# Top two of the gate with copy and guard on VectorE, and the output products of one layer in one slot

## Reference

```python
x = x + 0.5 * ffn(layernorm(x))      # first layer ("b" in the kernel)
x = x + attn(layernorm(x))           # attention
x = x + 0.5 * ffn(layernorm(x))      # second layer ("a" in the kernel)
```

```python
logits = normalize(h) @ normalize(sim) - sigmoid(gates)
gated = relu(logits)                         # experts with a positive logit are active
fallback = the 2 largest logits, where no expert is active
rw = softmax(where(active or fallback, gated, -inf))
q, k, v = (sum_e rw[e] * (h @ proj[e]) for each of the three)      # 64 wide
att = softmax(causal(q @ k.T / 8)) @ v
out = sum_e (att * rw[e]) @ o_proj[e]
```

## Time and profile before

| | |
|---|---|
| time, median of 3 runs | 4582.05 us (4581.81 to 4588.16) |
| profiled execution | 4587.97 us, its span on the core 4586.2 us |
| mean granted TensorE clock | 0.929 of full speed |
| TensorE busy (matmul) | 3939.6 us, 86% |
| VectorE busy | 4033.8 us, 88% |
| ScalarE busy | 3579.0 us, 78% |
| GpSimd busy | 3676.2 us, 80% |

### The profile page before, as it was taken

One profiled execution on the slowest core, in us unless ns is written; L12 is line 12 of the kernel. 1 busy time (PEld: TensorE's weight loads), 2 busy tenths in 40 slices (PEclk: granted clock), 3 DMA queues, 4 the chain that ended last, 5 costly groups with the idle time before them and its releaser, 6 DMA issues.

```text
span 4586.2 us, 93566 instructions
## 1 busy us (share of the span) xinstructions
PE 3939.6 (86%) x29004; PEld 3205.8 (70%) x29004; DVE 4033.8 (88%) x14021; ACT 3579.0 (78%) x9797; POOL 3676.2 (80%) x4414
## 2 busy tenths in 40 slices
PE   6678888898998899888898989888988988987777
PEld 5556777776777777777677777777777777765666
DVE  2389999989999998999999999999989899999992
ACT  2378878888887888888788878878888887877772
POOL 1567988888898888888888888988988898876650
PEclk8778999999999999999999999999999999989888
DMA  3111211112121111111112112111211111110011
GB/s 104 36 35 35 57 50 50 57 50 55 48 57 48 51 56 51 54 51 52 53 50 57 50 51 55 50 55 49 56 49 52 55 52 53 50 41 27 27 31 51
DMA packets 243941, 230.47 MB, mean 50 GB/s; under 512 B 27123, under 2 KB 176628, under 8 KB 243316
## 3 DMA queue, kind: packets, MB, share of 16 engines
q1 hardware_dynamic: 243444, 224.49, 17.5%
HBM read 214.98 MB, written 9.44 MB: 49 GB/s over the span
## 4 chain that ended last, share of the span: by engine, by line
POOL 50%; PE 20%; DVE 14%; issue 9%; ACT 6%; DMA 1%; SPq 0%; POOLq 0%; ACTq 0%; DVEq 0%
POOL HS L406 15%; POOL HL L1073 6%; POOL HL L1076 6%; POOL S L1075 6%; PE pQ L658 6%; POOL RB L419 5%; DVE M L990 4%; DVE HL L992 3%; PE pFa L602 3%; PE pST L642 2%; PE pFa L606 2%; PE pFb L626 1%; PE pO L699 1%; ACT HL L878 1%; PE pFa L544 1%
## 5 line engine op out<-in xcount | busy, mean ns | idle before, releaser
L658 PE MATMUL pQ<-wf_sb,HS 128*128 128x192 f32 x8192 | 1526.3, 343 | 196.6 <-POOL HS L406 172.4
L658 PEld LDWEIGHTS pQ<-wf_sb,HS 128*128 128x128 f32 x8192 | 1418.4, 201 | 250.2 <-POOL HS L406 151.0
L890 ACT ACTIVATE S<-S,M 128x512 f32<-128x512 f32 x1024 | 800.8, 782 | 2.9
L897 ACT ACTIVATE S<-S,lift 128x512 f32<-128x512 f32 x1024 | 787.7, 769 | 1.7 <-POOL lift L1064 1.7
L876 ACT COPY S<-pST 128x256 f32<-128x256 f32 x768 | 308.8, 402 | 456.7 <-issue 421.5
L406 POOL TENSOR_TENSOR HS<-hT_b,RB 128x1024 f32<-128x1024 f32 x240 | 575.7, 2399 | 5.0 <-PE pQ L658 3.3
L406 POOL TENSOR_TENSOR HS<-hT_a,RB 128x1024 f32<-128x1024 f32 x244 | 577.0, 2365 | 0.0
L885 ACT COPY PTs<-pST 128x512 f32<-128x512 f32 x1024 | 529.2, 615 | 4.1 <-PE pST L677 3.6
L1073 POOL TENSOR_TENSOR HL<-S,HL 128x512 f32<-128x512 f32 x384 | 491.2, 1279 | 45.6 <-ACT HL L878 45.5
L677 PE MATMUL pST<-ident,S 128*128 128x128 f32 x4096 | 508.6, 279 | 17.2 <-ACT S L873 12.4
L1075 POOL TENSOR_TENSOR S<-HL 128x512 f32<-128x512 f32 x384 | 493.1, 1284 | 30.1
(11 more groups left out here) (257 smaller groups left out, 8956.0 us busy)
## 6 DMA issues: line engine op xcount, KB each, us to landing
RB<-rows_b SPq DMA_DIRECT2D x384, 256.0 KB, 3.4
RB<-rows_a SPq DMA_DIRECT2D x384, 256.0 KB, 3.3
x_b<-in_x SPq DMA_DIRECT2D x64, 128.0 KB, 3.1
out_y<-y SPq DMA_DIRECT2D x64, 128.0 KB, 1.7
wf_sb<-in_wf SPq DMA_DIRECT2D x4, 768.0 KB, 7.0
rows_b<-rwT SPq DMA_DIRECT2D x64, 8.0 KB, 1.3
wof_sb<-in_wof SPq DMA_DIRECT2D x1, 1024.0 KB, 7.2
rows_a<-rwT SPq DMA_DIRECT2D x64, 8.0 KB, 1.4
```

What stands on the lines that cost most here:

```text
L658: mm = nc.tensor.matmul(pQ[:, 0:QKV], HS[:, k % 2, e, i, :], wf_sb[:, i, at:at + QKV], start=k + e + i == 0, stop=(k, e, i) == (3, 3, 1))
L890: nc.scalar.activation(S[:, r, :], S[:, r, :], ACT.Prelu, bias=M8[:, r, TH:TH + 1], scale=-1.0, alpha=1.0 / STEEP).then_inc(s_cut, 1)
L897: nc.scalar.activation(S[:, r, :], S[:, r, :], ACT.Exp, bias=lift[:, r:r + 1], scale=-STEEP).then_inc(s_gap, 1)
```

## The change

Pair is no longer a step of its own, and repl no longer has a slot of its own: VectorE does, in the slot of top, MAX8, the copy of the two largest (as a reduction over one element each), the guard nv (a negated maximum of the largest logit and a zero that stands in the widened buffer v8), and MATCH_REPLACE8. It waits for its own MAX8 before the copy, and for the copy before the replacement. GpSimd's gate makes one result less (four semaphore counts instead of five). For job a, TensorE issues all eight output products in slot 7; those of job b stay as they are.

```diff
@@ AT: the entries "pair" and "repl" go, for job a and for job b
-                self.v8 = sb(f"v8_{n}", P, 8)
+                self.v8 = sb(f"v8_{n}", P, 16)
...
-            if at := mine("pair"):
-                t, c = at
-                wait(eng, q["top"], t + 1)
-                ns.tensor_copy(J.mr8[:, 0:2], J.v8[:, 0:2]).then_inc(q["pair"], 1)
             if at := mine("gate"):
...
                 ns.tensor_scalar(J.pos[:], J.L[:], 0.0, None, ALU.is_gt).then_inc(g, 1)
-                ns.tensor_scalar(J.nv[:], J.v8[:, 0:1], 0.0, -1.0, ALU.max, ALU.mult).then_inc(g, 1)
-                wait(eng, g, 5 * t + 4)
+                wait(eng, g, 4 * t + 3)
...
@@ TensorE
-                if at := tile(J, "y", w, j, 1):
-                    t, c = at
-                    if isinstance(t, int) and (J.n, t) == ("b", 0):
+                if at := tile(J, "y", w, j, 1 if J.n == "b" else 0):
+                    t, c = at
+                    if J.n == "b" and t == 0:
                         pe.wait_ge(s_half, 1)
-                    wait(pe, q["read"], fill(J.n, w, j + 1))
-                    pe.wait_ge(s_mix, earlier(w, j + 1, MIXES.values()))
+                    of = j + 1 if J.n == "b" else j
+                    wait(pe, q["read"], fill(J.n, w, of))
+                    pe.wait_ge(s_mix, earlier(w, of, MIXES.values()))
                     for k in range(4):
                         nc.tensor.matmul(F[:, 0:D], RB2[:, k, :], wof_sb[:, k, :], start=k == 0, stop=False)
...
@@ VectorE, start
+                nc.vector.memset(jobs[n].v8[:], 0.0)
@@ VectorE, top
-                    nc.vector.max(J.v8[:], J.L[:]).then_inc(q["top"], 1)
-                if at := tile(J, "repl", w, j):
-                    t, c = at
-                    wait(dve, q["pair"], t + 1)
+                    nc.vector.max(J.v8[:, 0:8], J.L[:]).then_inc(q["top"], 1)
+                    dve.wait_ge(q["top"], t + 1)
+                    nc.vector.tensor_reduce(J.mr8[:, 0:2], J.v8[:, 0:2].unsqueeze(2), mybir.AxisListType.X, ALU.max
+                                            ).then_inc(q["pair"], 1)
+                    nc.vector.tensor_reduce(J.nv[:], J.v8[:, 0:16:8], mybir.AxisListType.X, ALU.max, negate=True
+                                            ).then_inc(q["guard"], 1)
+                    dve.wait_ge(q["pair"], t + 1)
                     nc.vector.match_replace(J.R[:], J.mr8[:], J.L[:], -BIG).then_inc(q["repl"], 1)
```

More of the change, by code:

```diff
@@ L62 @@
         "ctx_rec": 69, "ctx_norm": 71, "ctxT": 72, "x": 74, "x_sq": 76, "x_rstd": 77, "h": 78,
-        "hT": 79, "h_rinv": 79, "lg": 81, "shift": 82, "top": 83, "pair": 84, "repl": 85, "gate": 87,
+        "hT": 79, "h_rinv": 79, "lg": 81, "shift": 82, "top": 83, "gate": 87,
         "gate_exp": 88, "gate_em": 89, "gate_sum": 90, "rw": 91, "rwT": 92, "rw_st": 93, "hs": 96, "qkv": 104,
@@ L69 @@
         "x_ld": -51, "x_sum": -48, "x_sq": -46, "x_rstd": -45, "h": -44, "hT": -43, "h_rinv": -43,
-        "lg": -41, "shift": -40, "top": -39, "pair": -38, "repl": -37, "gate": -34, "gate_exp": -33,
+        "lg": -41, "shift": -40, "top": -39, "gate": -34, "gate_exp": -33,
         "gate_em": -32, "gate_sum": -31, "rw": -30, "rwT": -29, "rw_st": -28, "hs": -24, "qkv": -16, "qkT": -15,
@@ L271, in __init__ @@
                     "full", "read", "x_in", "x_sum", "x_sq", "x_eps", "x_rstd", "x_bias", "h_norm", "h_sq",
-                    "h_guard", "h_rinv", "shift", "top", "pair", "repl", "gate", "gate_exp", "gate_em", "gate_sum",
+                    "h_guard", "h_rinv", "shift", "top", "pair", "guard", "repl", "gate", "gate_exp", "gate_em", "gate_sum",
                     "gate_rec", "rw", "rw_st", "sc_max", "sc_exp", "sc_rec", "sc_norm")}
@@ L375, in layer @@
                 if ends:
-                    wait(eng, g, 5 * t)
+                    wait(eng, g, 4 * t)
                 eng.wait_ge(q["repl"], t + 1)
@@ L387, in layer @@
                 ns.tensor_tensor(J.ep[:], J.eg[:], J.pos[:], ALU.mult).then_inc(q["gate_em"], 1)
-                wait(eng, q["gate"], 5 * t + 5)
+                wait(eng, q["gate"], 4 * t + 4)
                 eng.wait_ge(q["gate_em"], 2 * t + 1)
@@ L740, in ffn @@
                     t, c = at
-                    act.wait_ge(q["gate"], 5 * t + 5)
+                    act.wait_ge(q["gate"], 4 * t + 4)
                     nc.scalar.activation(J.eg[:], J.L[:], ACT.Exp, bias=J.nv[:]).then_inc(q["gate_exp"], 1)
```

## The result

The changed kernel takes 4328.17 us (median of four runs, 4324.87 to 4329.89), the kernel before beside it 4585.10. The ratio is 0.944, 95% interval 0.942 to 0.945: 5.6% faster. The forecast was 4386 us, 4345 to 4500: the direction and the mechanism held, the gain was larger than the range allowed. The profiled execution took 4329.16 us with a span of 4327.4, against 4587.97 and 4586.2.

A forecast was written before the change was run, and what follows sets the result against it. No engine was full; a ring of waits between the engines bound the kernel. 4588.0 - 277.2 + 56 + 25 = 4391.8 us, the median 5.9 lower: forecast 4386 us, range 4345 to 4500.

The forecast's parts named there:

- the 25 us kept back for places that don't fit: Allowance for steady-part places where a resource does not fit: 1.8 us a window, 25 us over 14 windows.
- the 56 us for VectorE's added chain: Copy, guard and replacement in VectorE's gate: 0.46 us more a gate, x 122 = 56 us, bounds 43 to 85.
- 277.2 us listed: VectorE's steady waits, taken as winnable: nm_a for ScalarE's copy Sr 151.2 us, L1013 98.6 and L1005 27.4 for GpSimd's split.
- The walk: One tile followed with VectorE never waiting, 63.0 us of work: each resource fits, 1.5 to 3 us to spare at worst.
- The 0.22 us that I took off for before: VectorE's time a gate before the change: MAX8 0.07 us, replacement 0.08 for its value load plus 0.07.
- The ring: Waits, one turn per 67.2 us tile: GpSimd for MAX8, TensorE for the mix, ScalarE for scores, VectorE for Sr.
- B: VectorE's nm_a goes on waiting because TensorE is the true pace of ScalarE: 4512 us, chance 0.09.
- C: VectorE's split waits stay because GpSimd meets lift or a step waiting for ScalarE: 4487 us, chance 0.15.
- D: Slower: joint load of four engines sets the period, and VectorE's added chain lengthens every tile: 4638 us, chance 0.04.
- E: Each new VectorE reduction is held while a GpSimd instruction runs: 191 us more, 4577 us, no change; chance 0.03.
- Busy 50.50 of 50.50 us behind the stall: TensorE after its stall, in the tile with four of a window's six projections: the doubtful resource, 93% of 252 us.

The follow-up runs named there:

- part 2 alone: The kernel before with only the TensorE lines changed: all eight output products of job a in slot 7; 4470.94 us, ratio 0.975.
- the extra load: The kernel before with five unread reductions of a constant 128x128 tile added on VectorE in each gate's top slot; 4591.65 us, ratio 1.0017.

## Why the prediction was wrong

The forecast for the profiled execution was 4391.8 us, the measured 4329.16: the sum gave 196 us of gain, there were 259. The mechanism was right; two terms of the sum were mis-sized, both the same way: the 25 us kept back for places that don't fit (nothing of it was needed), and the 56 us for VectorE's added chain (its busy time rose by 18). The account closes on VectorE alone, since its span is its busy time and its idle time. Before, 4033.8 busy and 552.4 idle; after, 4051.8 and 275.6. So idle fell by 276.8 and busy rose by 18.0: 258.8.

- **The idle that goes: 277.2 us listed, 252.2 after my allowance; 276.8 in fact.** The step that failed is the allowance of "1.8 us a window" for places "where it does not" fit. The walk had found that each resource fits, with 1.5 to 3 us to spare, and the profile after says so too: L1013 and L1005 are not in the list of waits, nm_a waits 13.5 us in 14 windows. So 263.7 of the listed 277.2 us went. The other 13 are the net of two things that the sum put at nothing, as these stretches from the first MAX8 v_a to the 57th show, before and after:

```profile
384.74:4138.11 3753.37, 3334.74 (x25198) 2716.27 (x25197) 3475.29 (x12147) 3106.41 (x8523) 3269.60 (x3904) 0.95 0.19 52
382.69:3890.53 3507.84, 3199.67 (x25208) 2634.64 (x25209) 3490.54 (x12366) 3103.94 (x8520) 3224.15 (x3685) 0.99 0.20 55
```

  Between these two marks VectorE's idle time fell from 278.1 to 17.3 us, by 261: the 264 of the waits less 3 us of small gaps that the new chain brings. Ahead of the first mark it fell by 3 and behind the last by 13; I had taken ramp and tail as fixed. This term accounts for 25 of the 63 us.
- **The price of the chain: 56 us forecast, 43 to 85; busy time rose by 18.** The reductions took 155 and 145 ns, less than the copy's 169, and the guard hid wholly, so the chain holds VectorE 0.54 us and not 0.68. Zero for the guard was among my bounds, and I chose 0.11. I added up both traces, for each instruction from its start to the start of the next, less the idle time. The gate's own instructions (MAX8, copy, guard, value load, replacement) hold VectorE 34 us longer; with the 3 us of small gaps the chain costs 37 where I had 56. The 0.22 us that I took off for before was a little high: in job a the value load moved VectorE on by 0.02 us, not 0.08. The rest isn't the chain: the top-k's MAX8 passes take 17 us less. A pass that stands ahead of a wait is busy to its end, 0.41 us for 256 elements; with work behind it the next one starts after 0.33. Before, 146 of these passes stood ahead of an idle time, after only 23, and 123 x 0.08 is 10 us. My sum counted the waits and not this. The other 7 us are 2 to 3 ns on each pass over 256 elements, and why stays open.
- **The range.** Its lower end, 4345, was the sum with both terms at their low bounds (4588.0 - 277.2 + 43 - 5.9 = 4348). It held nothing for idle time outside the steady part or for a chain below 43, and the measured time is 17 us under it.
- **The ring** is borne out, by the changes of the waits and by the runs that cut it: GpSimd's wait for MAX8 gone, ScalarE's wait before the scores under 100 us, the first products at 389 ns (596 before) with 23 us of waits left of 177, VectorE full, GpSimd idle at lift. Cutting it in one place gives 234 or 114 us, in both 257.
- **Rivals.** B (nm_a stays) was wrong here, though with part 2 alone it is half true (64.8 of 144.8 us). C (split waits stay) is what part 2 alone shows, and was wrong for both parts. D fell with the extra load: +6.6 us where it asked for 100 or more. E holds for a copy, 81 us, and not for the reduction.
- **TensorE** was no bound. Busy 50.50 of 50.50 us behind the stall was, it seems, a queue catching up; with no stall it has 20 us idle in each window.

## What to carry to other kernels

When no engine is full and one part repeats, look for a ring: follow each engine's largest wait to the engine that ends it until you are back, and ask of every wait what stands behind it in the queue without needing it. One cut may bring most of what two bring, here 234 of 257 us. What can be won is about the idle time of the busiest engine in the steady part, here 277 us. To learn whether an engine sets the time, add a known load to it: +6.6 us for 114 us of work says no, +103 for about 124 says yes. Say where the load stands: ahead of the engine's own waits it hides, and a "no" there says nothing of the stretch behind them.

## What the runs showed of the hardware

- A copy of two float32 elements a row on VectorE (0.17 us alone) took up to 2.1 us beside GpSimd's products, 0.76 and 1.0 us at the median of the two jobs, and each of the 98 that took over 0.2 us ended within 0.03 us of a GpSimd instruction; a reduction with the same result took 155 ns in the mean of 64, beside the same products.
- On VectorE the guard starts 0.07 us behind the copy, for which it doesn't wait; an instruction that waits for the one ahead starts 0.19 to 0.20 us after it (1446.02 to 1446.22, and 1446.22 to 1446.41). Between long passes the copy by reduction costs 0.05 us (1443.28 to 1443.33).
- A MAX8 pass over 256 elements lasts 0.41 us and the next instruction starts after 0.33, if it waits for nothing. A wait behind such a pass that goes gives back these 0.08 us as well.
